# Macaron layer on one core: row places of their own, integer row numbers, and first turns of the merged stage written out by hand

## The reference

```python
def ffn(x):                      # x: 8192 x 128
    shared = (silu(x @ Wg.T) * (x @ Wu.T)) @ Wd.T
    probs = sigmoid(x @ router.T + bias)            # 8 routed experts
    scores, idx = top_k(probs, 2); scores /= scores.sum()
    return shared + sum(scores[k] * expert[idx[k]](x) for k in (0, 1))

def attention(x):                # 16 heads of 8, sequence of 256
    q, k, v = heads(x @ Wq.T + bq), heads(x @ Wk.T), heads(x @ Wv.T + bv)
    phi = lambda a: silu(a * 8 ** -0.25) + 1
    return (phi(q) @ (phi(k).T @ v)) @ Wo.T + bo

x = x + 0.5 * ffn(norm(x))
x = x + attention(norm(x))
x = x + 0.5 * ffn(norm(x))
```

## Time and profile before

| what | value |
|---|---|
| three runs | 773.49, 778.75, 779.38 us; median 778.75 |
| profiled execution | 779.15 us, of which span 777.2 us |
| busy in the span | PE 88%, DVE 72%, POOL 69%, ACT 60% |
| granted clock of PE, mean | 0.93 |

### The profile page before, as it was taken

How to read it: one execution, slowest core, us unless ns; L and a number is a source line. 1 busy time by engine, 2 the same in 40 slices (tenths; PEclk the granted TensorE clock), 3 DMA queues, 4 the chain that set the end, 5 groups by cost and what they waited for, 6 DMA issues and landing times. The chain is left out here.

```text
span 777.2 us, 17593 instructions
## 1 busy us (share of the span) xinstructions
PE 685.2 (88%) x4965; PEld 613.0 (79%) x4965; DVE 559.7 (72%) x1871; ACT 469.7 (60%) x863; POOL 538.9 (69%) x567
## 2 busy tenths in 40 slices
PE   4586867969999999989698999999889999999990
PEld 4475756859999998888566776777669999999990
DVE  6686877886555567767788998888787555576772
ACT  3335444526766776775666776776447767777760
POOL 3474777777777777777256676777777777777773
PEclk8588867989999999999889999999999999999995
DMA  8313221143354344553213211111324363477765
GB/s 275 105 52 121 76 65 52 53 118 115 103 166 131 106 128 151 155 171 112 76 54 96 70 42 43 46 45 46 88 76 121 110 175 109 137 213 221 222 200 171
DMA packets 63585, 89.72 MB, mean 115 GB/s; under 512 B 13188, under 2 KB 43908, under 8 KB 63492
## 3 DMA queue, kind: packets, MB, share of 16 engines
q1 hardware_dynamic: 46596, 53.70, 24.5%
q0 software_dynamic: 16896, 34.90, 13.3%
HBM read 46.42 MB, written 42.12 MB: 114 GB/s over the span
## 5 line engine op out<-in xcount | busy, mean ns | idle before, releaser
L634 POOL DMA_INDIRECT x_rows<-send,send_to x256 | 250.5, 979 | 139.6 <-issue 73.8
L646 POOL DMA_INDIRECT y_rows<-send,y_to x272 | 266.2, 979 | 85.5 <-issue 72.8
L1761 DVE TENSOR_TENSOR h<-silu_g,u_bank 128x512 f32<-128x512 f32 x136 | 93.2, 685 | 110.8 <-ACT silu_g L815 109.2
L790 ACT ACTIVATE slot_gu<-w_gu 128x1024 fp32r x130 | 137.7, 1059 | 40.2 <-issue 35.7
L1112 PE MATMUL y_bank<-w_dn,h 128*128 x1088 | 143.5, 275 | 0.4 <-DVE x L1328 0.3
L1112 PEld LDWEIGHTS y_bank<-w_dn,h 128*128 128x128 f32 x1088 | 132.8, 191 | 0.9 <-issue 0.8
L914 PE MATMUL g_bank<-xT_hi,slot_gu 128*128 128x256 f32 x260 | 84.9, 327 | 14.0 <-DVE xT_lo L1752 13.5
L1006 PEld LDWEIGHTS y_bank<-w_dn,h 128*128 128x128 f32 x512 | 65.5, 203 | 26.9 <-issue 26.3
L815 ACT ACTIVATE silu_g<-g_bank 128x512 f32<-128x512 f32 x136 | 79.0, 581 | 10.1 <-PE g_bank L916 9.9
L694 ACT ACTIVATE silu_g<-g_bank 128x512 f32<-128x512 f32 x64 | 38.0, 597 | 74.6 <-PE u_bank L916 41.6
L1006 PE MATMUL y_bank<-w_dn,h 128*128 128x128 f32 x512 | 67.4, 288 | 16.3 <-DVE x L1328 16.3
(11 more groups left out here) (252 smaller groups left out, 1486.9 us busy)
## 6 DMA issues: line engine op xcount, KB each, us to landing
send<-x_rows SPq DMA_DIRECT2D x130, 130.0 KB
y_pair<-y_rows SPq DMA_DIRECT2D x32, 512.0 KB
y_rows<-send,y_to POOLq DMA_INDIRECT x272
x<-x_in SPq DMA_DIRECT2D x16, 256.0 KB, 7.2
x_rows<-send,send_to POOLq DMA_INDIRECT x256, 2.3
out<-x SPq DMA_DIRECT2D x16, 256.0 KB
w_raw<-w_experts SPq DMA_DIRECT2D x15, 256.0 KB, 3.4
x_rows<-pad SPq DMA_DIRECT2D x16, 130.0 KB
```

The source lines that it names most:

```text
L634: pool.indirect_dma_start(x_rows, bass.IndirectOffsetOnAxis(ap=send_to[b % SEND_TO_RING][:, w, k:k + 1], axis=0), send[ring_of(f, t)][:, w ...
L646: pool.indirect_dma_start(y_rows, bass.IndirectOffsetOnAxis(ap=y_to[k][:, j:j + 1], axis=0), result_rows(f, s)[:, j, :], None).then_inc(y_ ...
L790: act.activation(slot_gu[n % 2][:].rearrange("p a n -> p (a n)"), w_gu[:, bass.ds(e, 1)].rearrange("p e a n -> p (e a n)").bitcast(F32), A ...
L1761: dve.tensor_tensor(h[par][0][:], silu_g[par][:], u_bank[par][:], ALU.mult).then_inc(slot_h_done, 1)
```

## The change

- `rows` gets 12 buffers of its own (ROW_RING = 12). The first six loads of a stage (ROWS_FIRST) wait for the tiles that fill the first slots to be sent, no longer for twelve tiles. From slot 12 on, `load_rows` waits for `y_sent` of the slot twelve before, that is, until its scatter has landed.
- The row's number is stored as an int32 in its word of the row. GpSimd reads the scatter's index from the row in place. `y_to`, its cast and its semaphore are gone. The weight is written by the routing's step 25 straight into `send`, and `row_tails` becomes `row_numbers`, a copy of numbers alone.
- `pick_places`: in the first slot stage ten tiles are added, at slots written out in ADD_AT, and LATE tiles are now six, added in turns 3 to 8. Their statistics are made in halves in two slots, and the normaliser's steps are spread by NORM_AT. Loads stand at place max(last slot + 13, add of the tile two before + 5 or + 12) for f = 0 or 1. Adds of f = 1 keep their slots.
- The merged stage's turns 0 and 1, and part of turn 2, are written out (`first_turns`) on TensorE, ScalarE and VectorE without late tiles, with tile 0's routing ahead; tile 1's norm is done by `variance`, a power on GpSimd and `shift_rows` (NEWTON = 1).

```diff
-ROW_RING = 6
+ROW_RING, ROWS_FIRST = 12, 6
...
-LEAVE = (15, 8)
-ADD_LEAVE, BETWEEN = (12, 8), (3, 2)
-LATE = 8
+ADD_AT = (42, 45, 48, 50, 53, 56, 58, 60, 63, 65)
+AFTER_ADD = (5, ROW_RING)
+LATE = len(ADD_AT)
+NORM_AT = {52: (3, 0, 2), 53: (3, 2, 4), 55: (3, 4, 8), 56: (3, 8, 10), 62: (7, 0, 4), 63: (7, 4, 6), 67: (7, 6, 10)}
+NEWTON = 1
 BY_VECTOR = (2, 3)
-LATE_TURN = {t: t - LATE for t in range(LATE, TILES)}
+LATE_TURN = {t: t - 7 for t in range(LATE, TILES)}
...
-NORMALISE_FROM = 56
+NORMALISE_FROM = 58
...
-        rows = [[send_pairs(f, ROWS_TILE + i // 4)[:, JS * (i % 4):JS * (i % 4 + 1), :] for i in range(ROW_RING)]
-                for f in range(2)]
...
-                adds.append(max(last_slot(f, t) + ADD_LEAVE[f], adds[t - 1] + BETWEEN[f] if t else 0,
-                                adds[t - Y_RING] + ROW_RING - 1 if t >= Y_RING else 0))
-                loads.append(adds[t] + LEAVE[f] - ADD_LEAVE[f])
+                if f == 0:
+                    adds.append(ADD_AT[t] if t < LATE else slots)
+                else:
+                    adds.append(max(last_slot(f, t) + 8, adds[t - 1] + 2 if t else 0, adds[t - Y_RING] + 5 if t >= Y_RING else 0))
+                loads.append(max(last_slot(f, t) + ROW_RING + 1, adds[t - Y_RING] + AFTER_ADD[f] if t >= Y_RING else 0))
...
                     i = entry(s)
                     row = sp.value_load(row_table[0:1, i:i + 1], min_val=0, max_val=most)
-                    wait_count(sp, y_out_done, n - ROW_RING + 1)
-                    sp.dma_start(rows[f][n % ROW_RING], x_rows[bass.ds(row, ROWS)].rearrange("(p j) d -> p j d", j=JS)
+                    wait_count(sp, y_sent[n % OUT_RING], y_sent_count(n - OUT_RING))
+                    sp.dma_start(rows[n % ROW_RING][:], x_rows[bass.ds(row, ROWS)].rearrange("(p j) d -> p j d", j=JS)
...
-                for t in range(ROWS_TILE + 2):
+                for t in range(BATCHES[f][BATCH_OF[f][COUNTED - 1]][-1] + 1):
                     sp.wait_ge(sent[ring_of(f, t)], sent_count(f, t))
-                for s in range(ROW_RING):
+                for s in range(ROWS_FIRST):
...
-                pool.wait_ge(y_to_done, n + 1)
                 pool.wait_ge(y_out_done, n + 1)
                 for j in range(JS):
                     pool.indirect_dma_start(
-                        y_rows, bass.IndirectOffsetOnAxis(ap=y_to[k][:, j:j + 1], axis=0),
+                        y_rows, bass.IndirectOffsetOnAxis(ap=rows[k][:, j, NUMBER:NUMBER + 1].bitcast(I32), axis=0),
...
+                if f == 1:
+                    for t in range(NEWTON, LAG_G):
+                        deviation(t)
...
+            def first_turns():
+
+                high((ATTN, 1, 2))
+                kvo_out(0)
+                k_silu(1, 0)
+                normalise(4, (0, 1))
+                k_silu(1, 1)
+                k_plus(1)
+                q_silu(1)
+                q_plus(1)
+                high((ATTN, 1, 3))
+                kvo_out(1)
+                k_silu(2, 0)
+                send_normalised(1, 0)
+                high((FFN, 1, 0))
+                normalise(4, (2, 3))
+                k_silu(2, 1)
+                k_plus(2)
+                q_silu(2)
+                send_second(1, 0)
+                q_plus(2)
+                normalise(5)
+                route_silu(1, 0)
+
             def middle():
-                for i in range(TURNS.stop):
+                first_turns()
+                for i in range(LAG_G, TURNS.stop):
...
+            def first_turns():
+
+                pe.wait_ge(y_out_done, slots)
+                key_value(0)
+                transpose_x((ATTN, 1, 2))
+                times_wo(0)
+                project(1, 0)
+                attend(0)
+                project(1, 1)
+                query(1)
+                key_value(1)
+                transpose_x((ATTN, 1, 3))
+                times_wo(1)
+                project(2, 0)
+                attend(1)
+                transpose_x((FFN, 1, 0))
+                project(2, 1)
+                router(1, 0)
+                query(2)
+                key_value(2)
+                ranks(1, 0)
+
             def middle():
-                for i in range(TURNS.stop):
+                first_turns()
+                for i in range(LAG_G, TURNS.stop):
...
-                            out=number_weight[:, :, ts[0] * SUB:ts[0] * SUB + n, 1], in0=picks(prob), scalar=0.5,
-                            in1=inv_total[:, 0:n].unsqueeze(1).to_broadcast([P, PICKS, n]), op0=ALU.mult, op1=ALU.mult)
+                        for i, t in enumerate(ts):
+                            wait_count(dve, sent[ring_of(f, t)], sent_count(f, t - SEND_RING))
+                            op = dve.scalar_tensor_tensor(
+                                out=send[ring_of(f, t)][:, :, :, WEIGHT], in0=prob[:, :, i * SUB:(i + 1) * SUB], scalar=0.5,
+                                in1=inv_total[:, i * SUB:(i + 1) * SUB].unsqueeze(1).to_broadcast([P, PICKS, SUB]),
+                                op0=ALU.mult, op1=ALU.mult)
...
-                    dve.tensor_copy(send[ring_of(f, t)][:, :, :, NUMBER:NUMBER + 2], number_weight[:, :, t * SUB:(t + 1) * SUB, :]
-                                    ).then_inc(row_tail_done, 1)
+                    dve.tensor_copy(send[ring_of(f, t)][:, :, :, NUMBER].bitcast(I32), number[:, :, t * SUB:(t + 1) * SUB]
+                                    ).then_inc(row_numbered, 1)
...
-                dve.tensor_copy(y_to[k][:], row[:, :, NUMBER]).then_inc(y_to_done, 1)
...
-                                norm_stats((ATTN, 1, t))
-                        q, i = NORM_OF[(ATTN, 1, t)]
-                        if f == 0 and i == len(NORMS[q]) - 1:
-                            if first_add(f, t) + 2 == s:
-                                normaliser(q, 0, NORM_STEPS // 2)
-                            if first_add(f, t) + 3 == s:
-                                normaliser(q, NORM_STEPS // 2, NORM_STEPS)
+                                norm_stats((ATTN, 1, t), (0,))
+                    for t in range(LATE if f == 0 else 0):
+                        if first_add(f, t) + 2 == s:
+                            norm_stats((ATTN, 1, t), (2,))
+                    if f == 0 and s in NORM_AT:
+                        t, first, last = NORM_AT[s]
+                        normaliser(NORM_OF[(ATTN, 1, t)][0], first, last)
...
+                q = NORM_OF[(FFN, 1, 0)][0]
+                mask_heads(0)
+                add_bias(0)
+                value(1, 0)
+                add_attention(0)
+                norm_stats((FFN, 1, 0))
+                value(1, 1)
+                normaliser(q, 0, 6)
+                mask_heads(1)
+                normaliser(q, 6, NORM_STEPS)
+                add_bias(1)
+                value(2, 0)
+                add_attention(1)
+                norm_stats((FFN, 1, 1))
+                variance(1)
+                value(2, 1)
+                route(1, 0, 0, RECIP_STEP)
+                shift_rows(1)
+                mask_heads(2)
+                route(1, 0, RECIP_STEP, ROUTE_STEPS)
+                row_numbers(1, 0)
+                add_bias(2)
...
-                        if i < LAG_G:
-                            normaliser(NORM_OF[(FFN, 1, i)][0], 0, NORM_STEPS)
-                        else:
-                            variance(i)
+                        variance(i)
                     if tr:
                         route(1, i - LAG_T, 0, MASK_STEP)
-                    if attn and i >= LAG_G:
+                    if attn:
```

More of the change, by code:

```diff
@@ L74 @@
 POWER_AFTER = 4
-STEPS_OF = [POWER_STEPS if items[0][:2] == (FFN, 1) and items[0][2] >= LAG_G else NORM_STEPS for items in NORMS]
+STEPS_OF = [POWER_STEPS if items[0][:2] == (FFN, 1) and items[0][2] >= NEWTON else NORM_STEPS for items in NORMS]
 STEPS_BEFORE = [sum(STEPS_OF[:q]) for q in range(len(NORMS) + 1)]
@@ L172, in part @@
             return a[:, starts[i]:starts[i] + widths[i]]
-        region_start, cell_expert, slot_number, falling, nobody_numbers = [part(counting, i) for i in range(1, 6)]
+        region_start, cell_expert, slot_number, falling = [part(counting, i) for i in range(1, 5)]
         stats = ring(3, "stats", [P, WIDEST, 3])
@@ L191, in macaron @@
         send_to = ring(SEND_TO_RING, "send_to", [P, PICKS, MOST], I32)
-        number_weight = sb("number_weight", [P, PICKS, tiles * SUB, 2])
+        number = sb("number", [P, PICKS, tiles * SUB], I32)
+        rows = ring(ROW_RING, "rows", [P, JS, ROW])
         pad = sb("pad", [P, ROUTED, JS, ROW])
@@ L540, in _ @@
                                  pad[:, e]).then_inc(padded, 16)
-                for s in range(ROW_RING, FIRST_SLOTS):
+                for s in range(ROWS_FIRST, FIRST_SLOTS):
                     load_rows(f, s)
@@ L1065, in slot_transpose @@
                 for j in range(JS):
-                    last = pe.transpose(slot_tr[n % 2][:, j * P:(j + 1) * P], rows[f][n % ROW_RING][:, j, 0:P], ident[:])
```

(5 more changed lines are left out.)

63 lines of the change are left out of this document (30 added, 33 removed).

## The result

The changed kernel takes 769.98 us (median of 10 runs, 768.92 to 772.37), the kernel before 777.01 (10 runs, 771.46 to 780.78). The ratio is 0.9923, 95% interval 0.9899 to 0.9946: faster by 0.8%, less than the 1% named in the forecast, but with an interval clear of 1. The forecast was 776, with 766 to 785; the sign and the range held, the middle lay 6 us too high. The profiled execution takes 771.06 us, 8.1 less than that of before.

A forecast was written before the change was run, and what follows sets the result against it. TensorE was taken as the limit, except some 14 us lost to pair loads and the merged stage's first turns, with GpSimd near its limit. Terms -2.4 - 3.8 + 3.0 = -3.2 against 779.15 gave 775.95, called 776; range 766 to 785.

The forecast's parts named there:

- Part 1: VectorE's cast of the row's number goes, 136 x 180 ns; claimed to count for nothing, 0 us.
- the dispatch's change: Dispatch of the first FFN, with copies of numbers half as wide: gains or loses under 0.5 us, taken as 0.
- Part 2: Start of the first slot stage: TensorE stalls for row loads that wait for landed scatters, slots 12 to 18; +6.6 us.
- Part 3: First slot stage, slots 40 to 67: earlier pair loads give back 9.0 of 10.4 us lost; -9.0 us.
- slack of 0.3 to 0.5 us a piece: First slot stage: each VectorE wait for a pair load reaches TensorE less some 0.3 to 0.5 us.
- Part 4: First turns of the merged stage: tile 0's mask comes sooner, -5.8 us to turn 3; whole merged stage -3.8 us.
- same-turn normaliser: Merged stage, turns 4 and 8: ScalarE waits for late tiles' normalisers made in the turn that applies them; +2.5 us.
- Part 5: Second slot stage: pair loads go back, VectorE waits seven times, 9.1 us in all; +3.0 us.
- cover at the end: End of the second slot stage: GpSimd's last scatters trail TensorE and cover part of the stall, guessed 0.6 us.
- (a): Faster: second-stage pair loads in time, late normalisers cost no wait; 770.5 or 766.6, middle 768.5; chance 0.27.
- (b): First turns gain nothing, ScalarE's send of tile 0's rows held by tile 1's kv copy; 782; chance 0.12.
- (c): Second slot stage: landing takes 4.2 us, loads half a us more, TensorE loses 15.4; 788; chance 0.10.

The follow-up runs named there:

- looped run: The changed kernel with the merged stage's first turns in the loop's order again and tile 1's ten-step normaliser: 776.05 us, ratio 0.9975.

## Why the forecast came out as it did

*Part 1, the cast.* Counted at nothing; the runs show nothing against it. The trace has no cast, and TensorE's undisturbed slot is still (281.95 - 256.72) / 10 = 2.523 us; no run takes this part back alone. The step that called the dispatch's change under 0.5 us stays open between 0 and the -2.5 seen, for the spread named above.

*Part 2, twelve places.* Right in mechanism and place: waits ahead of slot 12 and again behind the tables and the mixed weights. The term was too small, +6.6 for +8.2. Slot 18's transpose was put at 225.7 in a trace that starts its slots at 166.81, and came at 224.75 in one that starts them at 164.31: 1.6 later than forecast, counted from slot 0. The first stall was even a little smaller than its term, slot 12 late by 3.0 for 3.4. What was too small comes behind it: 1.0 is the tables, from whose first issue to slot 17's load pass 5.2 us (213.43 to 218.60) where 4.2 had passed, and 0.7 the landing ahead of slot 16's load, 3.0 us from the start of slot 4's second scatter for the 2.3 taken (POOL, then SP):

```profile
210.07 0.97 POOL L647 DMA_INDIRECT y_rows<-send,rows  x1 [0.30 <-issue]
```

```profile
213.05 0.33 SPq L505 DMA_DIRECT2D rows<-x_rows  x1
```

That the stall hangs on the landed scatters of twelve slots before is shown by sixteen places, which remove it.

*Part 3, pairs in the first stage.* -9.0 for -9.5 (-10.0 from slot 40 on): VectorE waits for no pair there. But the reason was given only in half. The loads are placed earlier, and that is one half; the other is that the stall of part 2 holds TensorE back to GpSimd's pace. With the stall gone a first wait of 3.7 us returns. I listed the two as independent terms; they share GpSimd's 2.54 us a slot, and that for this kernel the sum came out right is luck. (The slack of 0.3 to 0.5 us a piece is not what the forecast's own rows give, (12.1 - 10.4) / 8 = 0.2; nothing rests on it.)

*Part 4, the first turns.* -5.8 for the -7.4 between slot 67 and turn 3's first product (43.6 to 36.2 us). TensorE's lower clock vanished from the stretch, as the step had it. Of the 1.6 more 0.5 is VectorE's chain: the mask comes 26.9 us behind slot 67's transpose where it came 33.0, 6.1 us sooner for 5.6, and GpSimd's first rows 30.6 for 38.2. The other 1.1 lies behind the mask, from which to turn 3 pass 9.3 us for 10.6, while the forecast's sum leaves 0.2 for that piece (5.8 less 5.6): there the work that comes forward cost less than was charged against the clock. The looped run shows that the late tiles' leaving is 4.5 of the gain. From turn 3 to the end of the stage it lost 1.6 us, for the forecast's 2.0. For the same-turn normaliser the forecast took +2.5; a turn earlier gives 1.9 back. The two waits themselves are of 5 us, most of it behind other work.

*Part 5, pairs in the second stage.* Seven waits of 9.1 us in all were forecast (as listed they add up to 9.2), six of 7.9 came; TensorE lost 3.0 for 3.6 in this trace. The cover at the end was larger than guessed, 1.5 for 0.6, so that the part cost 1.5 us for 3.0. With loads three places ahead all of it, and 2 us of before, are gone: the price was the place alone. A pair load of the tail takes 4.4 us again, from 753.75 (SP) to 758.16 (DVE):

```profile
753.75 0.36 SPq L525 DMA_DIRECT2D y_pair<-y_rows  x1
```

```profile
758.16 0.69 DVE L1723 TENSOR_TENSOR x<-y_pair,x 128x512 f32<-128x512 f32 x1 [5.36 <-DMA y_pair<-y_rows]
```

The 3.2 us that the Trainium skill's formula gives ("DMA: Bandwidth & Descriptors", section "Anatomy of one DMA — SWDGE (gpsimd) path") is not borne out for these loads; it is a fit to transfers that GpSimd issues, and these are SyncE's. The Trainium skill's rule beside it, that a transfer's semaphore fires only when its last byte has landed, agrees with part 2 so far that slot 16's row load went out 2.0 us after GpSimd was done with slot 4's scatter (213.05 for 210.07 + 0.97); what passes in these 2 us no run shows.

*The rivals.* None came. (a) needed pairs in time and no wait for the late normaliser, and both waits are in the trace; that the time came near its 768.5 has other reasons: against the forecast's sum the trace has the dispatch at -2.5, the merged stage at -2.0, the second stage with its tail at -1.5 and the first stage at +1.1, -4.9 in all. The nearness is chance: the -2.5 is not shown to be the change's, and (a) named none of these terms but a part of the second stage's. (b) fell with the first turns. (c) fell with the waits' length.

## What to carry to other kernels

A buffer that is released by the last engine of a chain ties the first engine to that engine's backlog; count the backlog in places at the moment at which it is largest, here at the end of the dispatch, not in the steady state. When a wait goes, look for the slow queue that it hid: here one queue (GpSimd's scatters) could be met at the row places, at the pairs, or at the start of the next dispatch, and what the first stage had gained arrived in the merged stage whole only where all three were out of its way. An operation of 1 us that goes to a queue with a backlog can cost what is left of the backlog, and the clock behind the pause, not 1 us.

## What the hardware showed that I had not expected

Slot 0's transpose came between 159.9 and 166.8 us in thirteen traces with the same dispatch code, and GpSimd's first scatter already between 19.8 and 23.2 us, while the 27 slots from 40 to 67 took 68.4 to 68.7 us in all six kernels with twelve places. The second slot stage varied too, from 175.4 to 177.8 us where its pair loads stand alike. Where the spread of one kernel's runs arises is not shown, as each kernel has one trace; but single traces of two kernels can't be compared across the start. A long turn is not always a slow clock: of the changed kernel's two long turns one has a granted clock of 0.89, the other 1.00 at 15.84 us (465.45 to 481.29).
